# Mean squares by transposes and a VectorE sum, and the mask biases' table made in pairs of operations, in a four-layer cross-attention kernel

## Chip, cores and metric

One core of one Trainium2 chip. The metric is device microseconds of one execution of the whole program; a kernel's time is the median of its runs.

## What is computed

Four cross-attention layers in turn, over 8 batches of 512 tokens of 512 channels, with one context of 77 rows of 1024 channels for each batch. Layers 0 and 2 ("wide", kind A) have 16 heads of 64 and a bias that suppresses some context columns by a mask; layers 1 and 3 ("narrow", kind B) have 16 query heads of 32 over 4 key and value heads, and take an RMS norm of their input first:

```python
# wide
logits = einsum('bhqd,bhkd->bhqk', q, k) * scale
col_bias[:, token_indices_A] = (-SUPPRESS * (1 - mask_A))[:, None]
col_bias[:, token_indices_B] = (-SUPPRESS * (1 - mask_B))[:, None]
out = softmax(logits + col_bias) @ v
x = out @ Wo + bo + x
# narrow
inv = rsqrt(mean(x * x, axis=-1) + eps)
q = (x * inv * norm_w) @ wq
x = x + softmax(q k^T / sqrt(32)) v @ wo
```

## The kernel before

All products are made as three TensorE passes of a split number (a high part and a rest), so an eviction of PSUM is always a pair: ScalarE copies the high part out, then VectorE subtracts it and writes the rest.

**Context stage** (`context_part`). Nine rounds `j` over blocks of key and value weights. In each, TensorE makes four key banks and five value banks (`keys`, `values`), ScalarE and VectorE drain them (`drain_keys`, `drain_values`) and split the next weights (`split_weights`); SyncE stores keys and values to DRAM (L383, L388) and loads the next weights (L370). The value banks are four, so the fifth value block (`r == 4`) waits until VectorE has drained the first of its round (the semaphore `v_lo`). VectorE also makes the table `bias_s` of mask biases (L496 to L518): a chain of 39 small operations through the helper `link`, each waiting for the one before. It stands ahead of the first drain of round 0. GpSimd makes the constants that the table needs (`consts`), waits for the end of the chain (L1330), and only then zeroes `keys_s` and `vals_s`, whose memory overlaps the table's scratch. SyncE waits for that zeroing in round 3 (`begin(0)`), ahead of the first loads of `keys_s` and of the stores of that round's keys.

**Main loop** (`whole_block`). 130 steps `s`; a unit is one of four head groups of one batch of one layer, 32 units to a layer, 4 to a batch. In a step TensorE makes the scores of unit `s`, the queries of `s + 1`, the transposed probabilities of `s - 1` (`turn`, in three parts, four transposes each, L858), the weighted values of `s - 2` and, in some steps, a projection of a finished batch (`project`). VectorE takes the row maxima of four score tiles (L1155) and subtracts them (L1159), sums the exponentials (L1194), and writes rests. The order on each engine is written out by hand. Scores go through two banks: tile 2 waits for VectorE's subtraction of tile 0, tile 3 for that of tile 1.

**Mean squares of narrow layers.** ScalarE squares the four channel blocks of a batch and GpSimd adds them into `x_power` (channels down, tokens across). In the last step before the batch (`stats_at`, 16 times: 8 batches, 2 layers) TensorE multiplies `x_power` by the column `mean_w` (`stats`, L924: four float32 matmuls of one column), VectorE adds epsilon out of PSUM (`mean_squares`, L1202, 4 columns), and GpSimd takes the power -1/2 (`root`, L1327) for the scale of ScalarE's exponentials (L1046). Fourteen of the 16 stand in steps of a narrow layer, between the second and third part of the transposes; the other two stand in the last step of the wide layer before.

Of the kernel before, what the change touches and what calls it, by code (L numbers as in the profile page):

```python
# [20 lines left out]
F32 = mybir.dt.float32  # L21
# [6 lines left out]
P = 128  # L28
# [237 lines left out]
class Lasting:  # L266


    def __init__(self, nc, ctx):
        def sb(name, shape, dt):  # L270
            return ctx.enter_context(nc.sbuf_tensor(name, shape, dt))

        self.w_s = sb("w_s", [P, 4, 2, PART], F32R)
        self.x_s = sb("x_s", [P, 2, 2, XC, TOK], F32R)
        self.ident = sb("ident", [P, P], F32)
        self.mean_w = sb("mean_w", [P, 1], F32)
        self.mhalf = sb("mhalf", [P, TILES], F32)
        self.bias_s = sb("bias_s", [P, PAIRS, TILES, CTX], F32)  # L280
        self.bo = sb("bo", [P, PAIRS, XC], F32)
        self.nw = sb("nw", [P, PAIRS, XC], F32)
# [8 lines left out]
def context_part(nc, ctx, lasting, ctxT, kvw, k_scr, v_scr, k1_scr, v1_scr, x_in, wqA, boA, normB, masks, tokens,  # L291
# [19 lines left out]

    w_A, x_s, ident, mean_w, mhalf = lasting.w_s, lasting.x_s, lasting.ident, lasting.mean_w, lasting.mhalf
    bias_s, bo, nw = lasting.bias_s, lasting.bo, lasting.nw
# [142 lines left out]
    def vector(dve):  # L456
# [33 lines left out]
        def link(ins):  # L490

            links[0] += 1
            ins.then_inc(chain, 1)
            dve.wait_ge(chain, links[0])

        dve.wait_ge(consts, 5)  # L496
        dve.wait_ge(setup_loaded, 16 * 4)

        link(dve.tensor_scalar(mask_b[:, :, :], mask_b[:, :, :], 1.0, SUPPRESS * float(KIND_A.DH) ** 0.5, ALU.subtract,
                               ALU.mult))  # L500
        link(dve.tensor_copy(tok_f[:, 0, :], tok_i[:, :]))
        link(dve.tensor_scalar(tok_f[:, 1, :], tok_f[:, 0, :], float(CTX), None, ALU.add))
        for p in range(PAIRS):
            for which in range(2):
                hits = [(w, 4 * p + 2 * which + i) for w in range(2) for i in range(2)]
                for n, (w, i) in enumerate(hits):
                    if n == 0:
                        link(dve.tensor_scalar(cmp_t[which], iota_t, tok_f[:, w, i:i + 1], None, ALU.is_equal))
                    else:
                        link(dve.scalar_tensor_tensor(out=cmp_t[which], in0=iota_t, scalar=tok_f[:, w, i:i + 1],  # L510
                                                      in1=cmp_t[which], op0=ALU.is_equal, op1=ALU.max))

            link(dve.tensor_tensor(cmp_t[2], cmp_t[0], cmp_t[1], ALU.mult))
            link(dve.tensor_tensor(cmp_t[0], cmp_t[0], cmp_t[2], ALU.subtract))
            for t in range(TILES):
                link(dve.tensor_scalar(bias_s[:, p, t], cmp_t[0], mask_b[:, 0, t:t + 1], None, ALU.mult))
                link(dve.scalar_tensor_tensor(out=bias_s[:, p, t], in0=cmp_t[1], scalar=mask_b[:, 1, t:t + 1],
                                              in1=bias_s[:, p, t], op0=ALU.mult, op1=ALU.add))  # L518
        for j in range(NJ):
            for n in range(4):  # L520
                drain_keys(n, j)
            if j + 1 < NJ:
                split_weights(0, j + 1)
            else:
                split_late(1)
                split_late(2)
            for r in range(NV):
                drain_values(r, j)
            if j + 1 < NJ:
                split_weights(1, j + 1)  # L530
            if j + 2 == NJ:
                split_late(0)

    def gpsimd(pool):
        pool.wait_ge(ctx_lo, KC)
        pool.memset(ctx_raw[:, 0:3], 0.0).then_inc(cleared, 1)
        pool.memset(ident[:, :], 0.0).then_inc(consts, 1)
        pool.memset(mean_w[:, :], KIND_B.DH / D).then_inc(consts, 1)
        pool.memset(mhalf[:, :], -0.5).then_inc(consts, 1)
        pool.wait_ge(consts, 3)  # L540
        pool.wait_ge(cleared, 1)
# [48 lines left out]
def whole_block(nc, lasting, context_args, x_in, stream, k_scr, v_scr, k1_scr, v1_scr, wqA, woA, wqB, woB):  # L590

    with ExitStack() as ctx:
# [29 lines left out]
        stage = sb("stage", [P, 2, QUARTER], F32)  # L622
        w_s, x_s, ident, mean_w, mhalf = lasting.w_s, lasting.x_s, lasting.ident, lasting.mean_w, lasting.mhalf
        bias_s, bo, nw = lasting.bias_s, lasting.bo, lasting.nw
# [20 lines left out]
        t_mm, t_hi, t_lo = map(sem, ("t_mm", "t_hi", "t_lo"))  # L645
        acc_mm, o_hi, acc_out = map(sem, ("acc_mm", "o_hi", "acc_out"))
        rstd_ready, end_mm, end_out = sem("rstd_ready"), sem("end_mm"), sem("end_out")
        w_loaded = [sem("w_loaded0"), sem("w_loaded1")]
# [135 lines left out]
        def _(pe):  # L784
# [133 lines left out]
            def stats(gb):  # L918
# [4 lines left out]
                for t in range(TILES):  # L923
                    mm = pe.matmul(out[:, t:t + 1], x_power[:, t * P:t * P + P], mean_w[:, :],  # L924
                                   start=t == 0, stop=t == TILES - 1, skip_group_check=True)
                mm.then_inc(q_mm, 1)
# [222 lines left out]
        def _(dve):  # L1149
# [49 lines left out]
            def mean_squares(gb):  # L1199
                item = plan.q[("stats", gb)]  # L1200
                dve.wait_ge(q_mm, item + 1)
                dve.tensor_scalar(ms[:, gb % 2], q_bank[item % 2][:, 0:TILES], EPS * KIND_B.DH, None, ALU.add)\  # L1202
                   .then_inc(q_out, 1)
# [245 lines left out]
```

## Time and profile before

| what | value |
|---|---|
| median of 3 runs | 2080.31 us |
| the runs | 2079.71 to 2081.9 us |
| the profiled execution's span | 2080.3 us |
| TensorE matmuls busy | 2042.1 us, 98% |
| VectorE busy | 1389.7 us, 67% |
| ScalarE busy | 966.4 us, 46% |
| GpSimd busy | 644.7 us, 31% |

The span runs from the first to the last instruction, and is the profiled execution's own time: no other time is shown for it, and the median differs from it by less than 0.1 us. Times are microseconds from the span's start, so a row can be placed in its stage: the context stage lasts to about 270, the wide layer 0 to about 790, the narrow layer 1 to about 1160, the wide layer 2 to about 1695, and the narrow layer 3 to the end. In a timeline a number in brackets is the idle time of the engine ahead of the instruction, with what ended it.

### The profile page before, as it was taken

The numbers are of one execution on the slowest core, as the hardware profiler recorded it, in microseconds if no ns is written. First come the engines' busy times: TensorE is split into PE (matmuls) and PEld (weight loads), VectorE is DVE, ScalarE is ACT, GpSimd is POOL, SyncE is SP. The second block draws the span as 40 slices with busy tenths as digits, with TensorE's granted clock in tenths as the row PEclk, the third lists the DMA queues.
The fourth block names the chain that finished last, engine by engine and source line by source line (L and its number), as shares of the span: only waits on it lengthen the run. The fifth ranks groups of instructions, "written<-read, shape, count | busy, mean of one in ns | idle before, by whom it ended". The sixth has DMA issues, their size and how long they took to land.

```text
span 2080.3 us, 31294 instructions
## 1 busy us (share of the span) xinstructions
PE 2042.1 (98%) x11546; PEld 1764.4 (85%) x11546; DVE 1389.7 (67%) x2408; ACT 966.4 (46%) x1814; POOL 644.7 (31%) x519
## 2 busy tenths in 40 slices
PE   8999999999999998999999999999999989999998
PEld 8999988888888887788888888888888877888887
DVE  5322365775577557788888676557755775888886
ACT  3222354544355344555555454335443553555553
POOL 1000043311232244454443341223112533444441
PEclk9999999999999999999999999999999999999999
DMA  7889742222122222343333332212221232333332
GB/s 190 174 178 206 189 96 67 67 65 78 51 72 69 71 70 78 86 105 98 90 94 94 104 97 64 75 56 67 65 78 51 72 90 66 80 87 89 86 72 83
DMA packets 262537, 191.02 MB, mean 92 GB/s; under 512 B 197522, under 2 KB 199986, under 8 KB 259826
## 3 DMA queue, kind: packets, MB, share of 16 engines
q1 hardware_dynamic: 262386, 189.03, 35.6%
q8 instruction: 92, 1.51, 0.3%
q14 instruction: 59, 0.48, 0.1%
HBM read 132.66 MB, written 56.26 MB: 91 GB/s over the span
## 4 chain that ended last, share of the span: by engine, by line
PE 89%; DVE 6%; DMA 1%; ACT 1%; issue 1%; SPq 1%; POOL 0%; DVEq 0%; ACTq 0%; POOLq 0%
PE acc_bank L878 11%; PE acc_bank L261 8%; PE acc_bank L263 8%; PE acc_bank L262 8%; PE q_bank L836 8%; PE q_bank L840 8%; PE q_bank L838 8%; PE t_bank L858 7%; PE ctx_bank L261 3%; PE ctx_bank L262 3%; PE ctx_bank L263 3%; PE s_bank L799 2%; PE s_bank L261 2%; PE s_bank L796 2%; PE s_bank L802 2%; PE s_bank L263 2%
## 5 line engine op out<-in xcount | busy, mean ns | idle before, releaser
L1313 POOL TENSOR_TENSOR prob<-prob,rinv 128x1232 f32<-128x1232 f32 x128 | 288.5, 2254 | 1026.2 <-DVE rinv L1197 1026.2
L1055 ACT ACTIVATE q_s<-q_bank 128x512 fp32r<-128x512 f32 x192 | 115.0, 599 | 499.1 <-PE q_bank L840 494.8
L878 PE MATMUL acc_bank<-pT_s,vals_s 128*128 128x512 f32 x1024 | 337.8, 415 | 0.0
L1155 DVE TENSOR_REDUCE mx<-s_bank 128x4 f32<-128x308 f32 x512 | 240.2, 469 | 122.1 <-PE s_bank L263 63.2
L836 PE MATMUL q_bank<-x_s,w_s 128*128 128x512 f32 x768 | 318.9, 415 | 0.0
L840 PE MATMUL q_bank<-x_s,w_s 128*128 128x512 f32 x768 | 313.4, 408 | 0.0
L838 PE MATMUL q_bank<-x_s,w_s 128*128 128x512 f32 x768 | 312.8, 407 | 0.0
L261 PE MATMUL acc_bank<-o_s,w_s 128*128 128x512 f32 x752 | 303.6, 404 | 1.6 <-DVE o_s L1188 1.6
L263 PE MATMUL acc_bank<-o_s,w_s 128*128 128x512 f32 x752 | 296.7, 395 | 0.0
L262 PE MATMUL acc_bank<-o_s,w_s 128*128 128x512 f32 x752 | 296.7, 395 | 0.0
L1159 DVE TENSOR_TENSOR prob<-s_bank,mx 128x308 f32<-128x308 f32 x512 | 245.1, 479 | 27.4 <-DVE mx L1155 1.4
L1046 ACT ACTIVATE prob<-prob,rstd 128x308 f32<-128x308 f32 x256 | 140.5, 553 | 262.4 <-DVE prob L1159 247.1
L1182 DVE TENSOR_TENSOR pT_s<-t_bank,pT_s 128x512 fp32r<-128x512 f32 x256 | 175.8, 687 | 77.5 <-ACT pT_s L1069 77.5
L1211 DVE SCALAR_TENSOR_TENSOR x_back<-acc_bank,bo,x_back 128x512 f32<-128x512 f32 x64 | 47.8, 748 | 253.6 <-PE acc_bank L263 253.6
L878 PEld LDWEIGHTS acc_bank<-pT_s,vals_s 128*128 128x128 f32 x1024 | 190.6, 189 | 28.6
L1069 ACT ACTIVATE pT_s<-t_bank 128x512 fp32r<-128x512 f32 (+1 forms) x320 | 183.2, 590 | 40.0 <-PE t_bank L858 40.0
L858 PE MATMUL t_bank<-ident,prob 128*128 128x128 f32 (+1 forms) x1280 | 184.7, 273 | 1.2 <-DVE pT_s L1182 1.2
L1194 DVE TENSOR_REDUCE sums<-prob 128x16 f32<-128x1232 f32 x128 | 182.6, 1426 | 0.0
L858 PEld LDWEIGHTS t_bank<-ident,prob 128*128 128x128 f32 (+1 forms) x1280 | 154.7, 136 | 28.4 <-DVE pT_s L1182 1.6
L263 PEld LDWEIGHTS acc_bank<-o_s,w_s 128*128 128x128 f32 x752 | 141.0, 187 | 34.4
L261 PEld LDWEIGHTS acc_bank<-o_s,w_s 128*128 128x128 f32 x752 | 141.1, 188 | 33.8 <-DVE o_s L1188 3.2
L262 PEld LDWEIGHTS acc_bank<-o_s,w_s 128*128 128x128 f32 x752 | 141.3, 188 | 30.7
(107 smaller groups left out, 4095.5 us busy)
## 6 DMA issues: line engine op xcount, KB each, us to landing
stream<-x_back SPq DMA_DIRECT2D x128, 256.0 KB, 2.6
x_front<-stream SPq DMA_DIRECT2D x96, 256.0 KB, 3.3
x_back<-stream SPq DMA_DIRECT2D x96, 256.0 KB, 3.7
kvw_raw<-kvw SPq DMA_DIRECT2D x17, 1024.0 KB, 8.3
k_scr<-k_out SPq DMA_DIRECT2D x36, 308.0 KB, 10.4
keys_s<-k_scr SPq DMA_DIRECT2D x128, 77.0 KB, 2.5
v_scr<-v_out SPq DMA_DIRECT2D x8, 1024.0 KB
vals_s<-v_scr SPq DMA_DIRECT2D x512, 6.5 KB
```

The source lines that it names most:

```text
L261: pe.matmul(out, weights[0], moving[0], start=start, stop=False)
L262: pe.matmul(out, weights[0], moving[1], start=False, stop=False)
L263: return pe.matmul(out, weights[1], moving[0], start=False, stop=stop)
L836: pe.matmul(out, w[0], x_now[0], start=k == 0, stop=False)
L838: pe.matmul(out, w[0], x_now[1], start=False, stop=False)
L840: mm = pe.matmul(out, w[1], x_now[0], start=False, stop=k == XC - 1)
L858: mm = pe.transpose(t_bank[(3 * u + n) % 2][0:rows, t * P:t * P + P], p, ident[:, :])
L878: mm = pe.matmul(out, w, pT_s[:, part], start=i == mine[0] and part == 2 * n and w is v[0], stop=i == mine[-1] and w is terms[-1][0] and p ...
L1069: act.activation(pT_s[0:rows, 2 * n], t_bank[(3 * u + n) % 2][0:rows, :], ACT.Copy).then_inc(t_hi, 1)
L1155: dve.tensor_reduce(top, scored, AX_X, ALU.max).then_inc(s_max, 1)
L1159: dve.tensor_tensor(prob[:, slot, t].rearrange("q (h n) -> q h n", h=GH), scored, top.unsqueeze(2).broadcast_to([P, GH, CTX]), ALU.subtrac ...
L1313: pool.tensor_tensor(view, view, rinv[:, slot].unsqueeze(2).broadcast_to([P, TILES * GH, CTX]), ALU.mult).then_inc(p_norm, 1)
```

## The change

`mean_w` goes, and every tile that lies behind it in on-chip memory moves. `stats` makes four transposes of `x_power` against the identity, which fill all 512 columns of the query bank instead of 4. `mean_squares` becomes two VectorE operations with a wait between them: a sum of the 128 channels of each token, from 128x512 in PSUM to 128x4, and a multiply and add that makes the mean. The chain for `bias_s` becomes a generator: nothing of it runs in round 0, and in rounds 1, 2 and 3 VectorE runs two of its operations behind each key or value drain, until the 39 are used up (18 in round 1, 18 in round 2, 3 behind the first two key drains of round 3).

```diff
-        self.mean_w = sb("mean_w", [P, 1], F32)
...
             links[0] += 1
             ins.then_inc(chain, 1)
             dve.wait_ge(chain, links[0])
...
+            yield
+
+        def some(j):
+
+            if j in (1, 2, 3):
+                next(chained, None)
+                next(chained, None)
+
+        def setup():
+            dve.wait_ge(consts, 4)
+            dve.wait_ge(setup_loaded, 16 * 4)
...
+        chained = setup()
         for j in range(NJ):
             for n in range(4):
                 drain_keys(n, j)
+                some(j)
...
             for r in range(NV):
                 drain_values(r, j)
+                some(j)
...
-        pool.memset(mean_w[:, :], KIND_B.DH / D).then_inc(consts, 1)
...
                 for t in range(TILES):
-                    mm = pe.matmul(out[:, t:t + 1], x_power[:, t * P:t * P + P], mean_w[:, :],
-                                   start=t == 0, stop=t == TILES - 1, skip_group_check=True)
+                    mm = pe.transpose(out[:, t * P:t * P + P], x_power[:, t * P:t * P + P], ident[:, :])
                 mm.then_inc(q_mm, 1)
...
                 dve.wait_ge(q_mm, item + 1)
-                dve.tensor_scalar(ms[:, gb % 2], q_bank[item % 2][:, 0:TILES], EPS * KIND_B.DH, None, ALU.add)\
+                dve.tensor_reduce(ms[:, gb % 2], q_bank[item % 2][:, :].rearrange("q (t c) -> q t c", t=TILES), AX_X,
+                                  ALU.add).then_inc(ms_sum, 1)
+                dve.wait_ge(ms_sum, plan.b_batch(gb) + 1)
+                dve.tensor_scalar(ms[:, gb % 2], ms[:, gb % 2], KIND_B.DH / D, EPS * KIND_B.DH, ALU.mult, ALU.add)\
                    .then_inc(q_out, 1)
```

## Rows read from the trace of the kernel before

**Rows 1.** The page: the span, and TensorE's busy time, share and instructions.
```profile
span 2080.3 us, 31294 instructions
...
PE 2042.1 (98%) x11546; PEld 1764.4 (85%) x11546; DVE 1389.7 (67%) x2408; ACT 966.4 (46%) x1814; POOL 644.7 (31%) x519
```
**Rows 2.** Waits of TensorE over the span: total us, times, longest.
```profile
PE s_bank L261 <- DVE prob L1159: 15.6, 25, 2.5
```
**Rows 3.** Timeline of VectorE in the context stage: start, us, line, operation, tiles.
```profile
20.61 0.16 DVE L499 TENSOR_SCALAR mask_b<-mask_b 128x8 f32<-128x8 f32 x1
...
32.57 1.63 DVE L465 TENSOR_TENSOR k_out<-ctx_bank,k_out 128x308 fp32r<-128x308 f32 x4
...
104.33 0.48 DVE L465 TENSOR_TENSOR k_out<-ctx_bank,k_out 128x308 fp32r<-128x308 f32 x1 [2.37 <-ACT k_out L416]
```
**Rows 4.** Timeline of TensorE in the context stage, around its first long wait.
```profile
33.60 0.28 PE L262 MATMUL ctx_bank<-w_s,ctx_s 128*128 128x256 f32 x1
33.72 0.27 PE L263 MATMUL ctx_bank<-w_s,ctx_s 128*128 128x256 f32 x1
36.80 0.37 PE L261 MATMUL ctx_bank<-w_s,ctx_s 128*104 128x256 f32 x1 [2.81 <-DVE v_out L471]
...
41.07 0.46 PE L261 MATMUL ctx_bank<-ctx_s,w_s 128*128 128x308 f32 x1
```
**Rows 5.** Stretches: length, busy PE, PEld, DVE, ACT, POOL, then granted clock, DMA.
```profile
36.80:41.40 4.60, 4.60 (x26) 4.60 (x27) 0.94 (x3) 0.09 (x1) 0.00 (x0) 0.63 1.38 100
...
796.00:797.00 1.00, 1.00 (x5) 0.71 (x4) 0.77 (x2) 1.00 (x3) 0.00 (x0) 0.50 0.03 8
...
1700.00:1703.00 3.00, 3.00 (x17) 2.47 (x16) 1.54 (x4) 2.85 (x7) 0.00 (x0) 1.00 0.13 29
```
**Rows 6.** Timeline of SyncE's queue, and ScalarE's first key drain of round 4.
```profile
102.12 3.12 SPq L696 DMA_DIRECT2D keys_s<-k_scr  x4
...
107.33 8.84 SPq L383 DMA_DIRECT2D k_scr<-k_out  x4
...
128.26 0.43 ACT L416 ACTIVATE k_out<-ctx_bank 128x308 fp32r<-128x308 f32 x1 [1.22 <-PE ctx_bank L263]
```
**Rows 7.** Timeline of TensorE at the third mean squares of layer 1.
```profile
892.08 0.60 PE L858 MATMUL t_bank<-ident,prob 128*128 128x128 f32 x4
892.51 0.95 PE L924 MATMUL q_bank<-mean_w,x_power 128*128 128x1 f32 x8
893.33 0.60 PE L858 MATMUL t_bank<-ident,prob 128*64 128x128 f32 x4
...
898.78 0.30 PE L261 MATMUL s_bank<-keys_s,q_s 128*128 128x308 f32 x1
```
**Rows 8.** The page's groups: tiles, shapes, count, busy us, mean ns of one.
```profile
L1155 DVE TENSOR_REDUCE mx<-s_bank 128x4 f32<-128x308 f32 x512 | 240.2, 469 | 122.1 <-PE s_bank L263 63.2
L858 PE MATMUL t_bank<-ident,prob 128*128 128x128 f32 (+1 forms) x1280 | 184.7, 273 | 1.2 <-DVE pT_s L1182 1.2
L1194 DVE TENSOR_REDUCE sums<-prob 128x16 f32<-128x1232 f32 x128 | 182.6, 1426 | 0.0
```
**Rows 9.** Timeline of VectorE behind the third and the last mean squares.
```profile
895.07 0.15 DVE L1202 TENSOR_SCALAR ms<-q_bank 128x4 f32<-128x4 f32 x1
...
897.19 0.48 DVE L1155 TENSOR_REDUCE mx<-s_bank 128x4 f32<-128x308 f32 x1 [1.25 <-PE s_bank L263]
897.77 0.48 DVE L1159 TENSOR_TENSOR prob<-s_bank,mx 128x308 f32<-128x308 f32 x1
...
2015.75 0.48 DVE L1155 TENSOR_REDUCE mx<-s_bank 128x4 f32<-128x308 f32 x1 [1.26 <-PE s_bank L263]
```
**Rows 10.** Timeline of TensorE behind three of the four early mean squares.
```profile
794.17 0.41 PE L261 MATMUL s_bank<-keys_s,q_s 128*128 128x308 f32 x1 [2.52 <-DVE prob L1159]
...
856.26 0.41 PE L261 MATMUL s_bank<-keys_s,q_s 128*128 128x308 f32 x1 [0.56 <-DVE prob L1159]
...
1698.00 0.41 PE L261 MATMUL s_bank<-keys_s,q_s 128*128 128x308 f32 x1 [2.52 <-DVE prob L1159]
```

More of the change, by code:

```diff
@@ L310, in context_part @@
     banks = [early.enter_context(nc.psum_tensor(f"ctx_bank{i}", [P, 512], F32)) for i in range(8)]
-    w_A, x_s, ident, mean_w, mhalf = lasting.w_s, lasting.x_s, lasting.ident, lasting.mean_w, lasting.mhalf
+    w_A, x_s, ident, mhalf = lasting.w_s, lasting.x_s, lasting.ident, lasting.mhalf
     bias_s, bo, nw = lasting.bias_s, lasting.bo, lasting.nw
@@ L494, in link @@
             dve.wait_ge(chain, links[0])
[L496 to L518, printed above, removed]
@@ new lines, in link @@
+            yield
[6 more added lines that the diff above has]
+            dve.wait_ge(setup_loaded, 16 * 4)
+            yield from link(dve.tensor_scalar(mask_b[:, :, :], mask_b[:, :, :], 1.0, SUPPRESS * float(KIND_A.DH) ** 0.5, ALU.subtract,
+                                   ALU.mult))
+            yield from link(dve.tensor_copy(tok_f[:, 0, :], tok_i[:, :]))
+            yield from link(dve.tensor_scalar(tok_f[:, 1, :], tok_f[:, 0, :], float(CTX), None, ALU.add))
+            for p in range(PAIRS):
+                for which in range(2):
+                    hits = [(w, 4 * p + 2 * which + i) for w in range(2) for i in range(2)]
+                    for n, (w, i) in enumerate(hits):
+                        if n == 0:
+                            yield from link(dve.tensor_scalar(cmp_t[which], iota_t, tok_f[:, w, i:i + 1], None, ALU.is_equal))
+                        else:
+                            yield from link(dve.scalar_tensor_tensor(out=cmp_t[which], in0=iota_t, scalar=tok_f[:, w, i:i + 1],
+                                                          in1=cmp_t[which], op0=ALU.is_equal, op1=ALU.max))
+                yield from link(dve.tensor_tensor(cmp_t[2], cmp_t[0], cmp_t[1], ALU.mult))
+                yield from link(dve.tensor_tensor(cmp_t[0], cmp_t[0], cmp_t[2], ALU.subtract))
+                for t in range(TILES):
+                    yield from link(dve.tensor_scalar(bias_s[:, p, t], cmp_t[0], mask_b[:, 0, t:t + 1], None, ALU.mult))
+                    yield from link(dve.scalar_tensor_tensor(out=bias_s[:, p, t], in0=cmp_t[1], scalar=mask_b[:, 1, t:t + 1],
+                                                  in1=bias_s[:, p, t], op0=ALU.mult, op1=ALU.add))
@@ L537, in gpsimd @@
         pool.memset(ident[:, :], 0.0).then_inc(consts, 1)
-        pool.memset(mean_w[:, :], KIND_B.DH / D).then_inc(consts, 1)
         pool.memset(mhalf[:, :], -0.5).then_inc(consts, 1)
-        pool.wait_ge(consts, 3)
+        pool.wait_ge(consts, 2)
         pool.wait_ge(cleared, 1)
@@ L622, in whole_block @@
         stage = sb("stage", [P, 2, QUARTER], F32)
-        w_s, x_s, ident, mean_w, mhalf = lasting.w_s, lasting.x_s, lasting.ident, lasting.mean_w, lasting.mhalf
+        w_s, x_s, ident, mhalf = lasting.w_s, lasting.x_s, lasting.ident, lasting.mhalf
         bias_s, bo, nw = lasting.bias_s, lasting.bo, lasting.nw
@@ L646, in whole_block @@
         acc_mm, o_hi, acc_out = map(sem, ("acc_mm", "o_hi", "acc_out"))
+        ms_sum = sem("ms_sum")
         rstd_ready, end_mm, end_out = sem("rstd_ready"), sem("end_mm"), sem("end_out")
```

## The prediction

> **What bounds the kernel now.** I read the page's busy times first: TensorE is busy for 2042.1 of 2080.3 us [rows 1]. So a change can only win where TensorE waits, or by taking work from it. The next view is TensorE's waits. The largest entry is narrow-layer scores waiting for VectorE's subtraction, 15.6 us in 25 waits [rows 2]; the reader should see which engine is named, and that the list is short. The third view is the timeline around each place that the change touches, and there the answer differs from place to place.
>
> In the context stage VectorE starts the table at 20.61 and reaches the first key drain only at 32.57 [rows 3]; the first value drain stands behind it. TensorE's fifth value block waits 2.81 us for that drain, to 36.80 [rows 4]. Right behind it the granted clock of a stretch of 4.60 us is 0.63 on average [rows 5], so for part of it TensorE ran at 1.2 instead of 2.4 GHz; ahead of it stood that idle.
>
> At the 16 mean squares there are two kinds of place. Behind the first two of each narrow layer (four) VectorE is late and TensorE waits: 2.52 us at 794.17 and at 1698.00, 0.56 us at 856.26 [rows 10]; the second of the other layer looks the same. In the other twelve it is the reverse: VectorE's next instruction but one waits for TensorE's scores, 1.25 us behind the third of layer 1, 1.26 behind the last of layer 3 [rows 9], and no less in the ten between. There TensorE sets the pace, and VectorE has room.
>
> **The table, moved.** Without the chain VectorE drains round 0 as ScalarE delivers, long before TensorE needs the first value bank. TensorE's last start before the wait is at 33.72, 0.12 behind the one before; the fifth block would start at 33.84. It has 24 matmuls, and at 0.12 each they end at 36.72. Before, the next round begins at 41.07 [rows 4]. So 41.07 - 36.72 = 4.35 us come off, the wait and the half-speed matmuls behind it together. A few matmuls behind 41.07 are slow as well, which could add 0.2; the low end is the wait alone, 2.8, if the clock fell anyway. I take 4.35.
>
> Where do the 39 operations go? The chain takes 32.57 - 20.61 = 11.96 us [rows 3], 0.31 each, so a pair adds 0.6 us behind a drain. In rounds 1 to 3 a drain follows a block of 24 matmuls, 2.9 us at the pace of [rows 4], and takes about 0.5, so a pair fits between two; and the drain that the fifth value block waits for has four blocks of time, over 11 us. Cost nothing; with the cover gone it would be 12 us of VectorE.
>
> The chain's end moves to the second key drain of round 3, and with it GpSimd's zeroing and, on SyncE's queue, the wait ahead of the `keys_s` loads. Those start at 102.12 now [rows 6]. The second key drain of round 3 is at 104.33 [rows 3], the last operation ends near 105.1, and the zeroing stands behind that, so SyncE stands over 3 us; I take 4. Queued behind are four `keys_s` loads, two weight loads, and the stores of that round's keys, which begin at 107.33. These stores are wanted by ScalarE's first key drain of round 4 at 128.26 [rows 6], 21 us later. I cost this at nothing; all of it, should it reach TensorE, would be 4 us. The removed constant on GpSimd (0.1 us) is ahead of nothing that waits. That tiles move in memory has no row; I take zero.
>
> **The mean squares on TensorE.** The four one-column matmuls appear as eight instructions. From the first of them to the next part of the transposes is 893.33 - 892.51 = 0.82 us; the four transposes ahead of them, of the same shape and type as the new ones, take 892.51 - 892.08 = 0.43 [rows 7]. So 0.39 us less for each. Without the handover it could be 0.46 less. In the twelve places that TensorE paces: 12 x 0.39 = 4.7 us. In the four others the gain becomes a longer wait and is worth nothing.
>
> The Trainium skill, "TensorE: Matmul & The Clock Gate", section Part 4: PE-mode transpose, gives about 275 ns for a transpose inside a kernel. The mean duration of a transpose here is 273 ns [rows 8], which agrees, but four follow each other in 0.43 us, so the duration is not what one costs. If they did not overlap, the case is a rival below.
>
> **The mean squares on VectorE.** No row shows a sum of 128x512. Two of its kind bound it: 469 ns for 308 columns, 1426 ns for 1232 [rows 8]. The slope is (1426 - 469) / (1232 - 308) = 1.04 ns a column, which gives 469 + 204 x 1.04 = 680 ns; it is nearest to the first. The second operation costs what the old one did, 0.15 [rows 9], and the wait between them I estimate at 0.03 to 0.1. So VectorE gets 0.71 to 0.78 us more each time; the bounds are 0.5 and 1.5.
>
> In the twelve places the room must hold both the later VectorE and the earlier TensorE: 0.71 + 0.39 = 1.10 against 1.25. It just fits. And there is more behind it: VectorE's subtraction of tile 0 ends at 897.77 + 0.48 = 898.25 [rows 9], and TensorE asks for it at 898.78 [rows 7], so an overrun of up to 0.5 would not reach TensorE.
>
> In the four others TensorE waits for what VectorE does next [rows 10], so the 0.71 to 0.78 is on the path: 4 x 0.73 = 2.9 us. Behind the sum also wait GpSimd's root and, for that, ScalarE's exponentials; they need VectorE's subtractions too, which are late by the same 0.73, so it is not paid twice.
>
> The wait at 794.17 grows from 2.52 to about 3.6. The rows show the clock at 0.50 from 796 to 797 behind such a wait, and at 1.00 from 1700 to 1703 behind an equal one [rows 5], so whether it falls is not decided by the wait's length alone. A fall costs at most 4.60 x (1 - 0.63) = 1.7 us of TensorE's work. Two more falls, or two fewer, are 3.4 us either way at most; I take none.
>
> **Sum.** 2080.3 - 4.35 - 4.7 + 2.9 = 2074.1 us, 0.3% less. The span stands for the median, from which it differs by less than 0.1.
>
> **Rivals.** *The table's gain turns into another wait*: SyncE's stand in round 3, or the pairs behind the drains, reach TensorE. For it: the chain now ends 70 us later with a queue behind it. Against: 21 us of room. Price about 4.4, so 2078.5.
>
> *The transposes do not overlap in their place*: four at 273 ns are 1.09 us against 0.82, so 12 x 0.27 = 3.2 are added instead of 4.7 gained: 2080.3 - 4.35 + 3.2 + 2.9 = 2082.1. Against it: 0.43 for four in the row just ahead.
>
> *More falls of the clock* behind the longer waits at the start of each narrow layer: two more at the full price give 2077.5. For it: the idle there grows by 40%. Against: the matmuls there partly wait anyway, so a fall is not paid in full.
>
> *VectorE becomes the bound (slower).* Call what a batch adds to VectorE x. The four late places pay 4x. The twelve pay when x exceeds about 1.36 (1.25 less 0.39, and 0.5 to spare), then 12 (x - 1.36). With the gains of 4.35 + 4.7 the sum turns to a loss near x = 1.6, and at x = 2 it is 8 + 7.7 - 9.05 = +6.6, so 2086.9. For it: nothing but that no row shows this sum out of PSUM. Against: both bounds lie below 1.6.
>
> *VectorE's added time is hidden in the four places too*: 2080.3 - 4.35 - 4.7 = 2071.2. Against: TensorE waits for VectorE there.
>
> **Chances.** The forecast 0.74; the table's gain lost 0.08; no overlap 0.03; more clock falls 0.07; VectorE the bound 0.03; hidden everywhere 0.05. The range: the forecast's own ends are 2070.6 (4.55 for the table, 0.46 gained in each of the twelve, 0.5 paid in each of the four, and a fall fewer at 1.7) and 2076.9 (1.0 paid in each of the four, and a fall more). The low end holds the last rival; the high end is put at 2078.6, so that it holds the first. A measurement of this kernel can tell about 0.2% from no change, 4.2 us, so faster means below 2076.1: the forecast less 0.02 for its top end, the last rival, and 0.03 of the clock falls (one of them, or two paid by half, give 2075.8), together 0.80. Within 0.2%: that 0.02, the lost table, no overlap and the other 0.04 of the clock falls, 0.17. Slower: 0.03.
>
> **What would show it.** In the changed kernel's trace: TensorE's wait at 36.80 is gone, the granted clock is 1.00 there, and the second round begins near 36.7 instead of 41.07; the pairs stand behind drains of rounds 1 to 3 with idle left; SyncE's `keys_s` loads start near 102 (106 less 4). The new sum takes 0.68 us. Four transposes at a mean squares take 0.43. In the twelve places VectorE's idle before the next row maximum shrinks to about 0.1, and TensorE shows no new wait. At the first of each narrow layer TensorE waits about 3.6 instead of 2.5. The prediction fails if a wait of TensorE for VectorE appears in the twelve places, if the sum takes over 0.9 us, or if layer 0 starts less than 3.5 us earlier.

## The result and the profile after

The changed kernel takes 2069.39 us (2069.05 to 2070.4), the one before beside it 2080.22: a ratio of 0.9946 [0.9934, 0.9957], 10.8 us less. I had forecast 2074.1, with a low end of 2070.6. The sign was right and the size was too small; the rest of the document shows that the agreement in sign is luck.

The profiled execution has a span of 2067.3 us and a time of its own of 2069.05, so an execution takes some 1.75 us more than its span. Taking the span of before as its own time was therefore off by that much: its profiled execution took about 2082, near the slowest of the runs of before (2081.9).

The page of after, against [rows 1]:

```profile
span 2067.3 us, 31200 instructions
...
PE 2027.7 (98%) x11482; PEld 1762.3 (85%) x11482; DVE 1404.0 (68%) x2424; ACT 966.7 (47%) x1814; POOL 646.3 (31%) x518
...
L261 PE MATMUL acc_bank<-o_s,w_s 128*128 128x512 f32 x752 | 300.3, 399 | 0.2
L263 PE MATMUL acc_bank<-o_s,w_s 128*128 128x512 f32 x752 | 293.5, 390 | 0.0
L262 PE MATMUL acc_bank<-o_s,w_s 128*128 128x512 f32 x752 | 292.9, 390 | 0.0
```

and the same three groups on the page of before:

```profile
L261 PE MATMUL acc_bank<-o_s,w_s 128*128 128x512 f32 x752 | 303.6, 404 | 1.6 <-DVE o_s L1188 1.6
L263 PE MATMUL acc_bank<-o_s,w_s 128*128 128x512 f32 x752 | 296.7, 395 | 0.0
L262 PE MATMUL acc_bank<-o_s,w_s 128*128 128x512 f32 x752 | 296.7, 395 | 0.0
```

These are the projections, which the change does not touch: the same 2256 matmuls, of the same shape, each 5 ns shorter. What they cost is read from start to start. One batch's projections in layer 0 are 96 matmuls in a row; here are the second and the last of them in TensorE's timeline of before (start, duration):

```profile
336.44 0.39 PE L262 MATMUL acc_bank<-o_s,w_s 128*128 128x512 f32 x1
...
358.37 0.39 PE L263 MATMUL acc_bank<-o_s,w_s 128*128 128x512 f32 x1
```

and in that of after:

```profile
331.51 0.39 PE L262 MATMUL acc_bank<-o_s,w_s 128*128 128x512 f32 x1
...
352.85 0.39 PE L263 MATMUL acc_bank<-o_s,w_s 128*128 128x512 f32 x1
```

(358.37 - 336.44) / 94 = 233.3 ns before, (352.85 - 331.51) / 94 = 227.0 after. Every undivided batch of both wide layers gives these two values within 0.1 ns. Below, "pace" is this figure. 6.3 ns for 2256 matmuls would be 14 us, more than the whole result; and the stages follow it. From the unit whose sums end the first batch's start-up to the last one of the layer (VectorE's reciprocals of units 3 and 30, then 67 and 94) wide layer 0 takes 460.11 instead of 464.39 us and wide layer 2 461.66 instead of 465.17, 7.8 us together, in which no line was changed.

The rest of the difference lies where the forecast had put it, with gains and losses. The context stage ends 4.84 us earlier (the first unit's reciprocal at 278.10 instead of 282.94). TensorE's wait at 36.80 [rows 4] is gone: the fifth value block follows at once, and its 24 matmuls end at 36.62 where I had put 36.72.

```profile
33.68 0.28 PE L263 MATMUL ctx_bank<-w_s,ctx_s 128*128 128x256 f32 x1
33.80 0.28 PE L261 MATMUL ctx_bank<-w_s,ctx_s 128*104 128x256 f32 x1
...
36.62 0.30 PE L261 MATMUL ctx_bank<-ctx_s,w_s 128*128 128x308 f32 x1
```

But TensorE's waits grew, against 15.6 us in [rows 2] (waits of TensorE over the span):

```profile
PE s_bank L261 <- DVE prob L1169: 21.9, 24, 3.7
```

Behind the mean squares the timeline of TensorE now shows a wait of 3.71 us at the first of each narrow layer (2.52 in [rows 10]), 2.34 at the second (both layers), and one of 0.35 at the third and the fourth of layer 1, where [rows 7] had none; here are those of layer 1:

```profile
785.79 0.63 PE L261 MATMUL s_bank<-keys_s,q_s 128*128 128x308 f32 x1 [3.71 <-DVE prob L1169]
...
849.45 0.41 PE L261 MATMUL s_bank<-keys_s,q_s 128*128 128x308 f32 x1 [2.34 <-DVE prob L1169]
...
893.02 0.41 PE L261 MATMUL s_bank<-keys_s,q_s 128*128 128x308 f32 x1 [0.35 <-DVE prob L1169]
```

The new operations themselves, in the view of the tile `ms` (durations min, median, max, in ns):

```profile
L1212 DVE TENSOR_REDUCE ms<-q_bank x16: 678/679/691, 783.9 to 2001.7; 128x4 f32<-128x512 f32 x16
L1215 DVE TENSOR_SCALAR ms<-ms x16: 169/170/1243, 784.6 to 2002.4; 128x4 f32<-128x4 f32 x16
```

The sum is the 680 ns of the forecast. The small operation behind it is 0.17 in twelve places and 1.23 or 1.24 in four (846.36, 889.91, 933.22 and 1747.26). At the third mean squares VectorE's timeline shows one of the long ones:

```profile
889.19 0.68 DVE L1212 TENSOR_REDUCE ms<-q_bank 128x4 f32<-128x512 f32 x1
889.91 1.24 DVE L1215 TENSOR_SCALAR ms<-ms 128x4 f32<-128x4 f32 x1
891.18 0.69 DVE L1189 TENSOR_TENSOR pT_s<-t_bank,pT_s 64x512 fp32r<-64x512 f32 x1
```

and GpSimd's timeline what stands beside it:

```profile
889.83 1.30 POOL L1319 TENSOR_TENSOR w_s<-stage,w_s 128x512 fp32r<-128x512 f32 x1
891.23 1.02 POOL L1340 TENSOR_TENSOR rstd<-ms,mhalf 128x4 f32<-128x4 f32 x1
```

GpSimd's operation begins 0.08 us before VectorE's and ends at 891.13; VectorE's ends at 891.15. The same holds in the other three places (1747.17 with 1.28 beside 1747.26 with 1.23). Beside the first of each layer another operation of GpSimd runs, but it ends 0.16 us after the small one began (784.75 and 784.59), and that one takes 0.18; beside the other ten GpSimd does nothing. The old operation read PSUM; the new one reads and writes on-chip memory.

### The profile page after: what moved, and what is told of

It is laid out like the page before. It is cut to its first block, busy times and chain, and to the rows that moved or that the text cites. A ratio compares the mean times of both kernels' runs of the same rounds, so it can differ in the third digit from the quotient of the medians.

```text
span 2067.3 us, 31200 instructions
## 1 busy us (share of the span) xinstructions
PE 2027.7 (98%) x11482; PEld 1762.3 (85%) x11482; DVE 1404.0 (68%) x2424; ACT 966.7 (47%) x1814; POOL 646.3 (31%) x518
## 4 chain that ended last, share of the span: by engine, by line
PE 50%; issue 30%; POOL 11%; DVE 6%; ACT 1%; DMA 1%; SPq 0%; POOLq 0%; DVEq 0%; ACTq 0%
PE acc_bank L889 6%; POOL prob L1326 6%; PE t_bank L869 4%; PE acc_bank L261 4%; PE acc_bank L263 4%; PE acc_bank L262 4%; PE ctx_bank L261 4%; PE ctx_bank L262 4%; PE ctx_bank L263 4%; PE q_bank L847 4%; PE q_bank L849 3%; PE q_bank L851 3%; POOL x_s L1301 3%; PE s_bank L261 2%; POOL rest L1335 2%
## 5 line engine op out<-in xcount | busy, mean ns | idle before, releaser
L261 PE MATMUL acc_bank<-o_s,w_s 128*128 128x512 f32 x752 | 300.3, 399 | 0.2
L263 PE MATMUL acc_bank<-o_s,w_s 128*128 128x512 f32 x752 | 293.5, 390 | 0.0
L262 PE MATMUL acc_bank<-o_s,w_s 128*128 128x512 f32 x752 | 292.9, 390 | 0.0
L263 PEld LDWEIGHTS acc_bank<-o_s,w_s 128*128 128x128 f32 x752 | 141.1, 188 | 30.6
L261 PEld LDWEIGHTS acc_bank<-o_s,w_s 128*128 128x128 f32 x752 | 141.3, 188 | 28.7 <-DVE o_s L1198 1.8
L851 PEld LDWEIGHTS q_bank<-x_s,w_s 128*128 128x128 f32 x768 | 145.6, 190 | 23.2
```

The source lines that it names most:

```text
L261: pe.matmul(out, weights[0], moving[0], start=start, stop=False)
L262: pe.matmul(out, weights[0], moving[1], start=False, stop=False)
L263: return pe.matmul(out, weights[1], moving[0], start=False, stop=stop)
L851: mm = pe.matmul(out, w[1], x_now[0], start=False, stop=k == XC - 1)
```

## The experiments

The diffs of the whole change at the old addresses, of the sum kept in PSUM and of the mixed kernel start from the changed kernel, that of another pair from the mixed one, the others from before. An unused tile or a moved tile only shifts what lies behind it; "the moved tiles" are those of the second experiment. A time is a median in us, the ratio is to before measured beside it. In before `o_s` starts 32 bytes past a multiple of 256 from the start of the weights `w_s`; in after, at a multiple of 256.

**The whole change at the old addresses.** An unused tile of 4 bytes (32 with its padding) stands where `mean_w` was.

```diff
         self.ident = sb("ident", [P, P], F32)
+        sb("pad", [P, 1], F32)
         self.mhalf = sb("mhalf", [P, TILES], F32)
```

> The whole change, with an unused tile of one float a partition where mean_w stood, so that every tile lies where it lay before. If the unforeseen 4 us in each wide layer come from where the tiles lie: projection matmuls (read from o_s) start 234 ns apart again instead of 228, wide layers are as long as before, and the time is near 2079 (before, less 4.8 for the table, plus about 3 for the mean squares). If they come from the table or the mean squares themselves: 2069.4, and 228 ns stays.

Measured: 2081.4 us beside 2080.66, a ratio of 1.0004 [0.9995, 1.0013], and a pace of 233.2 ns. The changed code by itself gains nothing that can be told from noise; the whole 10.8 us hang on where the tiles lie.

**The kernel before, tiles moved.** Nothing of the change but the addresses.

```diff
-        self.mean_w = sb("mean_w", [P, 1], F32)
-        self.mhalf = sb("mhalf", [P, TILES], F32)
+        both = sb("mhalf", [P, TILES + 1], F32)
+        self.mhalf, self.mean_w = both[:, 0:TILES], both[:, TILES:TILES + 1]
```

> The kernel before with mean_w put into the unused end of mhalf's 32 bytes: same instructions, every tile behind it 32 bytes lower, as in the changed kernel. Theory of the addresses: projections 228 ns apart, about 8 us off in the wide layers and 2 in the narrow ones, 2070 to 2072. Rival (the addresses do nothing): 2080.2.

Measured: 2067.3, 0.9937 [0.9924, 0.9949], pace 226.9. That is more than the 8 to 10 us that I had expected, and 2.1 us below the changed kernel, though the two intervals overlap.

**One part alone, at the old addresses.** The table in pairs with the old mean squares; then the new mean squares with the old chain (each is its own part of the change, with the other part left out).

> The table alone in pairs behind the drains; mean squares and addresses as before. Both theories: the context stage 4.8 us shorter as in the changed kernel, all of it kept to the end: 2075.4. If a later wait takes some of it back: above 2076.

> The mean squares alone; table and addresses as before. My sum on record says 12 x 0.39 gained and 4 x 0.73 paid: 2078.4. By the changed kernel's trace (four of 16 small operations of 1.24 instead of 0.17 us, two more falls of the clock in each narrow layer) it is a loss of 2 to 4: 2082 to 2084.

Measured: the table 2077.16, 0.9982 [0.9973, 0.9991], 3.5 us less; the mean squares 2084.59, 1.0019 [1.001, 1.0028], 3.9 us more. They cancel, which is the first experiment's zero. The table gives less than the 4.8 that I had expected, but no later wait takes it back: behind the first reciprocal its profile is as long as that of before (1796.7 and 1797.3 us). What the table gives is settled further down.

**The sum kept in PSUM.** The whole change, but the small operation reads its sums from the bank, not from on-chip memory.

```diff
-                dve.tensor_reduce(ms[:, gb % 2], q_bank[item % 2][:, :]...
+                into = q_bank[item % 2][:, 0:TILES]
+                dve.tensor_reduce(into, q_bank[item % 2][:, :]...
...
-                dve.tensor_scalar(ms[:, gb % 2], ms[:, gb % 2], ...
+                dve.tensor_scalar(ms[:, gb % 2], into, ...
```

> The changed kernel, with the sum written to four columns of the same PSUM bank, so that the small operation behind it reads PSUM as it did before the change instead of SBUF. Theory: the four slow ones (1.24 us) wait for a GpSimd operation that holds a port to SBUF that both use; then all 16 take 0.15 to 0.17 and the time falls by 2 to 4, to 2065.5 to 2067.5. Rival (they wait for the sum or for a semaphore): 1.24 us stays in the same four places, 2069.4.

Measured: 2063.45, 0.9917 [0.9903, 0.993], 5.9 us less than the change. The view of `ms` in this run:

```profile
L1216 DVE TENSOR_SCALAR ms<-q_bank x16: 160/163/164, 784.7 to 1996.3; 128x4 f32<-128x4 f32 x16
```

and at the third mean squares, on VectorE's timeline and then on GpSimd's:

```profile
888.08 0.16 DVE L1216 TENSOR_SCALAR ms<-q_bank 128x4 f32<-128x4 f32 x1
```

```profile
888.00 1.29 POOL L1320 TENSOR_TENSOR w_s<-stage,w_s 128x512 fp32r<-128x512 f32 x1
```

All 16 take 0.16, here beside the same operation of GpSimd, again begun 0.08 us before. The time fell by more than the 2 to 4 us that I had expected. From the reciprocal before the second mean squares to the one behind it (unit 35 to 36, then 99 to 100) it is 10.47 and 10.46 us, against 12.59 and 12.39 in the change and 9.74 and 9.73 before; from unit 39 to 43 42.32 against 43.32. So the long ones were waits for GpSimd's operation, and they reached TensorE.

The Trainium skill, "SBUF — State Buffer", section "SBUF: two separate sides", says that VectorE, in a mode that uses two ports or with two inputs in on-chip memory, and GpSimd share one pair of ports, which the one that starts first holds for its whole instruction while the other blocks. The rows agree: 1.24 us beside GpSimd's 1.30, 0.16 without the read of on-chip memory; in which mode the small operation ran, no row shows.

**The mixed kernel.** Table in pairs, tiles moved; the first two batches of each narrow layer keep the one-column matmuls, the other twelve have the transposes with the sum in PSUM.

```diff
...
+                    if gb % B < 2:
+                        mm = pe.matmul(out[:, t:t + 1], x_power[:, t * P:t * P + P], mean_w[:, :], ...
+                    else:
+                        mm = pe.transpose(out[:, t * P:t * P + P], x_power[:, t * P:t * P + P], ident[:, :])
...
```

> Table in pairs, tiles moved (mean_w in mhalf's unused bytes), the old one-column matmuls for the first two batches of each narrow layer, where VectorE sets the pace, and transposes with a sum in PSUM for the other twelve. Theory: moved 2067.3, less some 2.3 for the table's wait, less 12 x 0.36 = 4.3: 2060 to 2062. If the twelve places don't gain: 2065.

Measured: 2061.21, 0.9906 [0.9892, 0.9919]; in a later run, beside the last experiment, 2060.51, 0.9901 [0.9885, 0.9918].

> The mixed kernel again, beside the one with pT_s moved: 2061.2 us by its earlier runs; all theories expect the same here.

**The table on the moved tiles**, with the old mean squares.

> The kernel before with all tiles 32 bytes lower (2067.3 us) and the table of mask biases made in pairs; the mean squares as in before. At the old addresses the table alone gave 3.5 us (2077.16 against 2080.66), about 1.5 of it a clock fall in the context that the moved kernel without the table did not have. If the gains add without that fall: 2067.3 - 2.3 = 2065 us; if the whole 3.5 adds: 2063.8; if the table's gain needs the old addresses: 2067.

Measured: 2063.8, 0.9918 [0.9904, 0.9932]: 3.5 us below before with the tiles moved, as at the old addresses. The mixed kernel lies 2.6 us below this one, not the 12 x 0.38 = 4.6 that its twelve places gain (see below): in the profiles the narrow layers are 4.5 us shorter, but wide layer 2 is 1.7 longer, at its first unit behind the start-up, where TensorE waits for ScalarE some 1.0 us more. Why, no run shows.

A part of the table's gain in the profile of after does not come with every execution: in the profile of before with the tiles moved TensorE waits 2.09 instead of 2.81 us, and behind the wait the granted clock does not fall. TensorE's timeline in that run:

```profile
36.38 0.37 PE L261 MATMUL ctx_bank<-w_s,ctx_s 128*104 128x256 f32 x1 [2.09 <-DVE v_out L471]
```

and the stretch (length, busy PE, granted clock, DMA share, GB/s) that had 0.63 in [rows 5]:

```profile
36.80:41.40 4.60, 4.60 (x38) 1.00 1.40 102
```

The first reciprocal is there at 280.41, against 282.94, with the old chain. So of the 4.84 us of the two profiles some 2.5 come and go with the clock and the wait's length. It is not the addresses: in the second sweep below, whose tiles are moved as well, wait and fall are as in before, while five profiles with the context's tiles at the old places have no fall:

```profile
36.51 0.37 PE L261 MATMUL ctx_bank<-w_s,ctx_s 128*104 128x256 f32 x1 [2.79 <-DVE v_out L471]
```

```profile
36.80:41.40 4.60, 4.60 (x28) 0.63 1.38 99
```

Eleven of the profiles have the old chain. In four of them the wait is 2.74 to 3.22 us, that stretch has 0.63, and the first reciprocal is at 282.6 in the mean; in seven the wait is 1.06 to 2.10, the stretch has 1.00, and it is at 280.8. In the eight with the table in pairs it is at 278.4. So the table gives 4.2 us in an execution with the fall and 2.5 in one without, 3.1 in the mean of the profiles.

**Which tile, and where.** First `o_s` with the three tiles behind it, 32 bytes up and 96 bytes up (an unused tile ahead of `o_s`, taken from the unused one behind); `x_s` and `ident` 32 bytes up; and `o_s` 16 bytes up on the moved tiles.

```diff
+        sb("pad", [P, 8], F32)
         o_s = sb("o_s", [P, 2, 8, TOK], F32R)
...
-        sb("unused", [P, 128], F32)
+        sb("unused", [P, 120], F32)
```

> The kernel before with only o_s, xsq, x_power and rest 32 bytes higher (o_s then starts at an odd multiple of 64 bytes; it began 32 bytes past one), everything else in place. Theory: the moved kernel gains because the projections stream o_s from a multiple of 64 bytes; then projections fall from 234 to 228 ns apart here too, 2068 to 2071. Rival 1: a multiple of 128 bytes is needed; then 234 ns and 2080.7. Rival 2: another tile (keys, probabilities, x_front) makes the gain; then 234 ns is not the point and the time stays 2080.7.

> The kernel before, with o_s, x_power, xsq and the tiles behind them 96 bytes higher, so that o_s starts on a multiple of 128 bytes; nothing else is moved. In before, where o_s starts 32 bytes past a multiple of 64 and of 128, a projection matmul took 233.6 ns in the wide layers; 32 bytes higher (a multiple of 64, not of 128) 229.5 ns; 32 lower (a multiple of 128) 227.5 ns. If the multiple of 128 gives the last 2 ns: 227.5 ns, and 752 x 3 matmuls x 2 ns = 4.5 us less than the 2071.99 of o_s 32 higher, of which the narrow layers have shown part only, so about 2069 us. If something else that was moved down with o_s gives it (keys, probabilities): 229.5 ns and 2072 us.

> The kernel before with mean_w allocated ahead of x_s instead of behind it: x_s and ident start 32 bytes past a multiple of 64, all other tiles stay. Theory: any operand that TensorE streams in 512 columns pays some 6 ns a matmul at such a start; the 2304 query matmuls read x_s, so up to 13 us more where they set the pace: 2088 to 2094, query matmuls 234 ns apart instead of 228. Rival (only o_s or its neighbours matter): 2080.7.

> The kernel before with all tiles 32 bytes lower (2067.3 us, 227.5 ns a projection matmul), in which o_s alone begins 16 bytes further in, so that its columns start 16 bytes past a multiple of 64. If every start off a multiple of 64 costs the same extra step of reading: 233 ns a projection matmul and 2077 to 2080 us. If the time goes by how far the start is off (16 of 32): about 230.5 ns and 2073. If only 32 bytes past a multiple matters: 227.5 ns and 2067.3.

Measured: 32 up 2071.99, 0.9958 [0.9946, 0.9971], pace 228.9. 96 up 2078.57, 0.9991 [0.9982, 1.0], pace 232.3: my theory of a multiple of 128 bytes fell here. `x_s` moved: 2079.76, 0.9996 [0.9987, 1.0005]; the query matmuls of the narrow layers went from 229.8 to 233.0 ns (mean of neighbouring starts), but the time did not follow, and the 8 to 14 us more that I had expected did not come. Nor is their pace a matter of `x_s` alone: with the tiles moved, where `x_s` and `w_s` stay, it is 231.3. 16 up on the moved tiles: 2076.65, 0.9983 [0.9974, 0.9991], pace 231.7.

**Sweeps of `o_s`.** In the next two kernels each of the 16 batches of the wide layers keeps its `o_s` at a start of its own, so one profile holds 16 of them; the first goes by 32 bytes from before, the second by 8 bytes from the moved tiles. The diff is the first one's.

```diff
...
+        o_tile = sb("o_s", [P, 16 * TOK + 128], F32R)
+        starts = {0: [0, 160, 320, 480, 128, 288, 448, 96], 2: [256, 416, 64, 224, 384, 32, 192, 352]}
+
+        def o_part(u, h, c):
+            layer, b = u // UNITS, u // GROUPS % B
+            at = (starts[layer][b] if layer in starts else 0) // 4 + (8 * h + c) * TOK
+            return o_tile[:, at:at + TOK]
...
```

> The kernel before, in which each of the 16 batches of the wide layers keeps its outputs o_s at a start of its own, 0 to 480 bytes above the old one in steps of 32, in mixed order; x_power, xsq and rest lie 512 bytes higher, nothing else is moved. If the start of o_s alone sets the pace of the projections: one value for each start, the same at the starts that were measured one by one (0: 233.2 ns from start to start in a batch, +32: 229, +96: 232.3), so a curve that shows with what period the good starts return; the start 480 higher, 32 short of the next 512, gives 226.9 if the period is 512 or less. If other tiles set it: all 16 batches the same.

> The kernel before with its tiles 32 bytes lower (mean_w beside mhalf), in which each of the 16 batches of the wide layers keeps its outputs o_s at a start of its own, 0 to 120 bytes above in steps of 8, in mixed order. If the start of o_s sets the pace: 226.9 ns at 0, 231 to 232 at +16, 233.2 at +32, 229 at +64, and the steps between show whether it is a matter of a few good starts or a slope. If other tiles set it: 226.9 in all 16.

Measured, one run each: 2078.3 and 2076.5 us, and one pace for each start (table below). The groups of two neighbouring batches in the first sweep, with starts 480 (537.5 to 559.1) and 128 (604.9 to 627) above the old one:

```profile
L262 PE MATMUL acc_bank<-o_s,w_s 128*128 128x512 f32 x32 | 12.4, 389 | 0.0
...
L262 PE MATMUL acc_bank<-o_s,w_s 128*128 128x512 f32 x32 | 12.7, 396 | 0.0
```

A batch next to another, the same code and the same stage, and 7 ns apart. The starts 224 and 480 give 226.9 both, 32 and 288 give 229.0 and 228.9, 0 and 256 give 233.3 and 233.4: over the 512 bytes tried the curve repeats after 256.

**The weights moved instead.** Is it the start of `o_s`, or its distance from the weights? The same sweep, with `w_s` 128 bytes higher (and with it `x_s` and `ident`, and `bias_s` by 64, which the projections do not read).

```diff
+        self.mean_w = sb("mean_w", [P, 1], F32)
+        self.mhalf = sb("mhalf", [P, TILES], F32)
+        self.bo = sb("bo", [P, PAIRS, XC], F32)
+        self.nw = sb("nw", [P, PAIRS, XC], F32)
         self.w_s = sb("w_s", [P, 4, 2, PART], F32R)
...
-        self.mean_w = sb("mean_w", [P, 1], F32)
-        self.mhalf = sb("mhalf", [P, TILES], F32)
...
-        self.bo = sb("bo", [P, PAIRS, XC], F32)
-        self.nw = sb("nw", [P, PAIRS, XC], F32)
...
```

> The sweep of o_s in steps of 32 bytes, with the weights w_s, the inputs x_s and ident 128 bytes higher (the four small tiles mean_w, mhalf, bo and nw lie ahead of them) and o_s where it was. The sweep with the weights at the old place gave one curve with a period of 256 bytes: 226.9 ns where o_s starts 128 past a multiple of 256 (starts 224 and 480 higher), 229.0 at 192 (32 and 288 higher), 233.2 to 234.3 elsewhere. If the start of o_s itself counts: the same curve at the same starts. If its distance from the weights counts (a multiple of 256 was the best): the curve goes 128 bytes along, so 226.9 at the starts 96 and 352 higher and 229.0 at 160 and 416, and 233 at 224, 480, 32 and 288.

Measured, in one run of 2078.66 us: the curve went along, by the 128 bytes of the move. The starts 160 and 416 now give 228.9 (233.2 before), 224 gives 232.3 (226.9 before), and 96 and 352, whose projections stand in two halves at the narrow layers' beginning, 226.7 to 227.8 (232.2 to 233.3 before). The group of start 160 (402.2 to 424) beside that of 480 (537.8 to 559.5):

```profile
L262 PE MATMUL acc_bank<-o_s,w_s 128*128 128x512 f32 x32 | 12.4, 388 | 0.0
...
L262 PE MATMUL acc_bank<-o_s,w_s 128*128 128x512 f32 x31 | 12.2, 394 | 0.0
```

All values by (start of `o_s` - start of `w_s`) modulo 256, in ns, over the runs above; two batches where two are given:

```
distance   sweep by 32    sweep by 8   weights moved   one place in all batches
0          226.9, 226.9   227.0        227.3           226.9 (after, and before moved)
16                        231.7                        231.7
32         233.3, 233.4   233.4        233.2, 233.2    233.2 (before)
64         229.0, 228.9   228.9        228.9, 228.9    228.9
96         233.3, 233.3   233.4        233.4, 233.4
128        232.8                       232.2, 232.3    232.3
160        234.3, 234.3                234.1, 234.1
192        233.2, 233.2                233.3, 233.4
224        233.5, 233.3                233.3, 233.2
8, 24, 40, 48, 56 (sweep by 8):        233.3, 234.1, 232.0, 233.2, 231.8
72, 80, 88, 104, 112, 120 (the same):  234.9, 231.1, 231.5, 233.3, 231.1, 235.1
```

(The values at distance 0 of the moved weights, at 128 of the first sweep and at 24 and 88 are means of batches that are projected in two halves. Those at 224 of the first sweep, 48 and 112, and 96 of the moved weights are of the seventh batch of a layer, whose projections are interrupted once; that pause is left out.) Of the 20 places tried two are good, 0 and 64; 8 bytes above 0, or on either side of 64, it is 231.8 or more: no slope. Where a place was measured more than once, the values agree within 0.6. The weights were moved to one other place only.

The Trainium skill, "TensorE: Matmul & The Clock Gate", section "Step-by-step: what each phase is for", says that TensorE reads streamed operand and weights through two independent ports, so that loading the next weights takes nothing from the running matmul. Here the place of the one against the other is worth 6.3 ns of 233; the measurement decides, though no run shows how the two meet.

**Is `o_s` all of it?** The kernel before with `o_s` alone at distance 0, 224 bytes up.

```diff
+        o_s = sb("o_s", [P, 16 * TOK + 128], F32R)[:, 56:56 + 16 * TOK].rearrange("p (h c n) -> p h c n", h=2, c=8)
```

> The kernel before with o_s alone 224 bytes higher (x_power, xsq and rest 512 higher, which keeps their places in 256), so that o_s starts 128 past a multiple of 256, as it does when all tiles are 32 bytes lower. If the start of o_s is all that the move of the tiles gave: 226.9 ns a projection matmul in the wide layers and about 2067.5 us, as with all tiles moved (2067.3). If the other tiles' places gave part of the 13 us: 226.9 ns and 2069 us or more.

Measured: 2069.05, 0.9946 [0.9932, 0.9959], pace 226.9. One tile's place gives 11.3 us. By the expectation's own terms 2069 or more speaks for a part of other tiles, but the 1.75 us more of all tiles moved lie within the two intervals, so whether another tile has a part stays open.

**Another pair.** The mixed kernel with the transposed probabilities `pT_s` at distance 0 from the values `vals_s` (128 before).

```diff
-        sb("unused", [P, 128], F32)
+        sb("unused", [P, 64], F32)
...
+        sb("pad0", [P, 32], F32)
         pT_s = sb("pT_s", [P, 6, TOK], F32R)
+        sb("pad1", [P, 32], F32)
```

> The mixed kernel (table in pairs, tiles 32 bytes lower, one-column matmuls for the first two batches of each narrow layer, transposes summed in PSUM for the others; 2061.21 us) with the transposed probabilities pT_s 128 bytes lower, so that their distance from the values vals_s, which these matmuls load as weights, becomes a multiple of 256 (it was 128 past one); nothing else has its place in 256 changed. In the sweeps a projection matmul whose operand lay 128 past took 232.3 ns, at a multiple 226.9. If the same holds for the 1024 probability-by-value matmuls: 1024 x 5.4 ns = 5.5 us less at most, about 2056; half of it if the wide layers, where they alternate with score matmuls, don't feel it, about 2058.5. If it's a matter of long runs of matmuls alone: 2061.2.

Measured: 2058.97, 0.9894 [0.9879, 0.9908], the fastest of all, 1.5 us below its base on the same chip. But the reason that I gave does not show: in the narrow layers these matmuls follow each other at 229.8 ns here and 230.7 in the base (mean of neighbouring starts), 0.9 apart and not 5.4, and those layers did not become shorter. The stages that did are the context (1.3 us, of which 0.8 is within what two profiles of the base differ by) and wide layer 2 (0.8), so this is not the distance rule, and its cause is open.

## Why the prediction was wrong, step by step

**The step that failed** is the last sentence of the table's part: "That tiles move in memory has no row; I take zero." It is a term of -11 to -13 us (the two runs with before's code and other addresses), larger than the whole forecast, and without it the change gains nothing. It had no row in before alone, as the sentence says; but then it was an unknown without a bound, and the range should have been wider for it. The front names the move of every tile behind `mean_w`, so the question was there.

**The sum of the rest** was forecast at -4.35 - 4.7 + 2.9 = -6.2, and measured at the old addresses at +0.7 [-1.0, +2.7] (the interval of the ratio times 2080.7).

**The table**: 4.35 forecast, 4.84 in the two profiles, 3.5 timed, at the old addresses and at the new. The mechanism was right to the row, wait gone and the block's end within 0.1. Mis-sized was the half-speed stretch: I took [rows 5] for what every execution has, and of the eleven profiles with the old chain only four have it, those with the longest waits; the profile that the forecast was read from has the latest first reciprocal of all (282.94). The timed 3.5 lies between the low end that I named, the wait alone, 2.8, and my value. SyncE's `keys_s` loads start at 101.80 where I had 102, and nothing there reached TensorE.

**The twelve places**: 0.39 us each forecast. Between kernels with the tiles moved and the table in pairs, four units around such a place take 42.70 with the old mean squares and 42.32 with the transposes summed in PSUM, so 0.38, right. Four transposes take 0.43 in the change (to the next part of the others), as forecast; they overlap, and that rival fell:

```profile
886.64 0.60 PE L935 MATMUL q_bank<-ident,x_power 128*128 128x128 f32 x4
887.07 0.60 PE L869 MATMUL t_bank<-ident,prob 128*64 128x128 f32 x4
```

In the change itself two of the twelve lost 0.43 and 0.45 against before instead, the third and fourth of layer 1: there the small operation took 1.24, and TensorE's new wait of 0.35 is the failure that I had named.

**The four early places**: 0.73 us each forecast. The first of each layer cost 0.78 and 1.04 with the sum in PSUM and 0.67 and 1.18 in the change (five units around each, against the table alone on the moved tiles), near the forecast, and their wait of 3.71 is the 3.6 that I had put. With the sum in PSUM the second ones cost 0.73 and 0.73 (10.47 - 9.74, 10.46 - 9.73), right to the hundredth. In the change they cost 2.85 and 2.66. The step that failed is "The second operation costs what the old one did, 0.15": it now reads on-chip memory beside GpSimd. 1.24 - 0.17 = 1.07 of it is the wait for GpSimd, and the 1.05 and 0.86 that remain stand with a fall of the clock behind the longer wait of TensorE. The change at the old addresses tells the two apart: there the second place of layer 3 has the wait (2.36) and no fall, and costs 11.53 - 9.74 = 1.79, which is 0.73 + 1.07 and nothing more. The stretches of the change (length, busy PE, granted clock, DMA share, GB/s):

```profile
786.80:787.80 1.00, 1.00 (x5) 0.50 0.03 7
800.00:801.00 1.00, 1.00 (x6) 0.50 0.00 0
851.00:852.00 1.00, 1.00 (x4) 0.50 0.10 15
1687.50:1688.50 1.00, 1.00 (x5) 0.50 0.20 47
1701.00:1702.00 1.00, 1.00 (x6) 0.50 0.00 0
1752.00:1753.00 1.00, 1.00 (x4) 0.50 0.19 36
```

and those of before:

```profile
786.80:787.80 1.00, 0.92 (x7) 1.00 0.18 40
796.00:797.00 1.00, 1.00 (x5) 0.50 0.03 8
...
859.50:860.50 1.00, 1.00 (x6) 1.00 0.09 13
1700.00:1701.00 1.00, 1.00 (x8) 1.00 0.06 11
1711.00:1712.00 1.00, 1.00 (x4) 0.50 0.14 20
```

Six stretches at 1.2 GHz around the four early mean squares instead of two; those of 786.80, 851, 1687.50 and 1752 stand right behind the waits that had grown. The same code at the old addresses has four of them. I took none more, and in layer 3 of before I had read 1700 to 1703 as a place without a fall, where the fall came at 1711. The rival of more falls was right in what happens, but the total does not show it, because the larger term hid it. With the sum in PSUM the stretches behind the second mean squares are gone, and 5.9 us with them, more than the four waits of 1.07 by themselves. So corrected, the new mean squares are worth 0.35 us (2063.45 against the 2063.8 of the table alone on the moved tiles), not the 1.8 of the forecast, which the two intervals do not tell from nothing.

**VectorE as the bound** and **no gain from the table** did not come; the added time was not hidden in the four places either.

## What to carry to other kernels

Before a small gain or loss is put down to an edit, compare the pace of instructions that the edit did not touch; if a tile was added or taken away, run the old code at the new addresses, since here 32 bytes were worth 11 us and the edit nothing. Where a long run of matmuls sets the time, its streamed tile's distance from the weights is worth a sweep, and one profile can hold it if each batch has its own start. A small VectorE operation that moves from PSUM to on-chip memory can get a new neighbour, GpSimd, and then last as long as what GpSimd is doing, as here in four of 16 places. And before a price is read from one profile, other profiles of the same code show how often the row is there.

## What the hardware showed that I had not expected

A 128x512 projection matmul of this kernel takes 226.9 ns from start to start where the streamed tile's distance from the weights is a multiple of 256 bytes, 228.9 at 64 past one, and 231 to 235 at the other 18 places tried; moving the weights by 128 bytes moves the curve by as much. The query matmuls show a step in the narrow layers (229.8 to 233.0 at distance 32) that the time does not feel, and the probability matmuls hardly any (230.7 to 229.8 from 128 to 0). The granted clock behind the long wait of the context stage fell in four of the eleven profiles that have this wait, so a fall seen once is a bound and not a price.
